# Attention of the first and last layer: values trail by three blocks; the ternary steps divided anew over the engines

## What is computed

```python
# layers 0 and 3, 16 heads of 16, 1024 tokens, per batch
scores = q @ k.T / 4
attn = softmax(where(causal, scores, -inf))
out = attn @ v            # layer 3 also multiplies by w_out and adds b_out

# layer 2, weights of the feed-forward branch, once for the whole run
def ternary_quant(w_fp32, g=64):
    w = w_fp32.astype(bfloat16)
    w_g = w.reshape(-1, g)
    scale = clip(mean(abs(w_g), axis=-1, keepdims=True), 1e-08, None)
    q = clip(round(w_g / scale), -1, 1)
    w_hat = (q * scale).reshape(w.shape)
    return w + stop_gradient(w_hat - w)
```

## Time and profile before

| what | value |
|---|---|
| runs, median (lowest to highest) | 4462.45 us (4454.85 to 4469.24), 3 runs |
| profiled execution, time | 4468.33 us |
| its span, first to last instruction | 4466.6 us |
| mean granted TensorE clock | 0.902 of full speed |
| PE busy | 3635.4 us, 81% |
| DVE busy | 2574.3 us, 58% |
| ACT busy | 1904.4 us, 43% |
| POOL busy | 850.4 us, 19% |

### The profile page before, as it was taken

One profiled execution on the slowest core, in us unless ns is written; L12 is line 12 of the kernel. 1 busy time (PEld: TensorE's weight loads), 2 busy tenths in 40 slices (PEclk: granted clock), 3 DMA queues, 4 the chain that ended last, 5 costly groups with the idle time before them and its releaser, 6 DMA issues. The chain is left out here.

```text
span 4466.6 us, 62749 instructions
## 1 busy us (share of the span) xinstructions
PE 3635.4 (81%) x23244; PEld 2181.8 (49%) x23244; DVE 2574.3 (58%) x5320; ACT 1904.4 (43%) x2923; POOL 850.4 (19%) x1022
## 2 busy tenths in 40 slices
PE   5776786768768888888893888987988888898897
PEld 3424333235166373554732666655653653663672
DVE  5756665647465454554546455455665665764764
ACT  2262461542656566464662434343126126216206
POOL 3012111120122030110302223232311220220220
PEclk8987897888889999898995989998999999999999
DMA  5411403214140000000002000002000000000000
GB/s 187 123 40 62 128 29 120 75 62 123 34 152 1 5 25 6 24 1 29 1 6 78 1 29 29 5 24 78 1 1 29 1 1 29 1 1 29 1 1 10
DMA packets 147087, 177.10 MB, mean 40 GB/s; under 512 B 16384, under 2 KB 123392, under 8 KB 146688
## 3 DMA queue, kind: packets, MB, share of 16 engines
q1 hardware_dynamic: 139008, 153.81, 10.9%
q0 software_dynamic: 6144, 16.79, 1.1%
q10 hardware_dynamic: 1632, 2.49, 0.2%
HBM read 126.40 MB, written 51.38 MB: 40 GB/s over the span
## 5 line engine op out<-in xcount | busy, mean ns | idle before, releaser
L708 DVE TENSOR_REDUCE arena<-ps 128x2 f32<-128x1024 f32 (+3 forms) x768 | 698.8, 953 | 170.6 <-PE ps L676 96.4
L906 ACT ACTIVATE arena<-ps 128x1024 f32<-128x1024 f32 (+3 forms) x768 | 576.6, 811 | 162.9 <-PE ps L813 111.8
L989 DVE TENSOR_TENSOR arena<-arena,tri 128x256 f32<-128x256 f32 x512 | 210.2, 423 | 354.5 <-ACT arena L906 325.2
L813 PE MATMUL ps<-arena 64*128 64x512 f16 (+3 forms) x1536 | 261.7, 355 | 163.3 <-ACT arena L906 99.0
L830 PE MATMUL ps<-arena 128*17 128x512 f32 (+3 forms) x3072 | 350.8, 531 | 6.4 <-DVE arena L989 4.1
L906 ACT ACTIVATE attention<-ps 128x1024 f32<-128x1024 f32 (+3 forms) x384 | 287.5, 810 | 142.7 <-PE ps L813 142.6
L2557 ACT ACTIVATE arena<-ps 128x256 f32<-128x256 f32 x192 | 63.6, 381 | 620.2 <-PE ps L2499 574.9
L813 PEld LDWEIGHTS ps<-arena 64*128 64x128 f16 x1536 | 71.1, 94 | 521.8 <-ACT arena L906 404.4
L830 PE MATMUL ps<-attention,live 128*33 128x512 f32 (+3 forms) x1536 | 290.8, 502 | 0.0
L676 PE MATMUL ps<-arena 64*128 64x512 f16 (+3 forms) x1536 | 238.2, 336 | 54.0 <-DVE arena L708 47.3
L1158 PE MATMUL ps<-gated_parts,weight_parts 128*128 128x256 f32 x1536 | 216.2, 298 | 30.4 <-DVE operands L1258 30.4
(11 more groups left out here) (324 smaller groups left out, 7094.6 us busy)
## 6 DMA issues: line engine op xcount, KB each, us to landing
arena<-w_experts SPq DMA_DIRECT2D x128, 256.0 KB
acc<-sums SPq DMA_DIRECT2D x16, 1024.0 KB, 5.9
x_next<-sums SPq DMA_DIRECT2D x16, 1024.0 KB, 8.5
arena<-slots_x SPq DMA_DIRECT2D x32, 512.0 KB, 4.6
slots_y<-arena SPq DMA_DIRECT2D x32, 512.0 KB, 4.3
sums<-acc SPq DMA_DIRECT2D x24, 512.0 KB, 2.9
making<-basis SPq DMA_DIRECT2D x16, 768.0 KB, 6.5
slots_x<-arena SPq DMA_DIRECT2D x1, 4096.0 KB, 29.5
```

The costliest lines, as they stand in the source:

```text
L708: dve.reduce_max(a.mp[:, 2 * j:2 * j + 2, qt, c], out[:, :, 0:w], AX.X).then_inc(self.pair_out, 1)
L813: last = pe.matmul(m.ps[:, 4 + 2 * (v % 2) + odd, q0:CH], a.k[half, pair, kt * P:(kt + 1) * P], a.q[half, pair, c * CH + q0:(c + 1) * CH], ...
L906: act.activation(a.p[:, v % ring, :, q0:CH], m.ps[:, b:b + 2, q0:CH], ACT.Exp, scale=HD ** -0.5).then_inc(exped, 1)
L989: dve.tensor_tensor(diag, diag, keep, ALU.min).then_inc(masked, 1)
```

## The change

In `attention` the lag becomes 3 where a group has two pairs (layers 0 and 3). The finishing pieces and `keep_sums` count from it and move one block later too.

In `ternary_weights` GpSimd's part goes, and VectorE does the last two steps for all three parts. ScalarE spreads the scale of a part over its 2048 columns into a new bf16 buffer, `f.spread`, and VectorE multiplies by that in place of the broadcast. There is one such buffer, so ScalarE waits for the part ahead (`ready`) before it fills it again.

```diff
@@ attention
-    lag = 2
+    lag = 3 if pairs == 2 else 2
@@ ternary_weights, VectorE
-                step(dve.tensor_scalar(f.sc[:, :], f.sc[:, :], 1e-8, None, ALU.max))
+                dve.tensor_scalar(f.sc[:, :], f.sc[:, :], 1e-8, None, ALU.max).then_inc(scale_made, 1)
+                dve.wait_ge(scale_made, i + 1)
...
-                dve.tensor_tensor(g3(q1), g3(q1), bc(f.sc[:, :]), ALU.mult).then_inc(scaled, 1)
-                dve.wait_ge(scaled, i + 1)
-                if i == last_part:
-                    dve.wait_ge(ready, last_part)
-                    step(dve.tensor_tensor(q1, q1, wb, ALU.subtract))
-                    dve.tensor_tensor(q1, q1, wb, ALU.add).then_inc(ready, 1)
-
-        @block.gpsimd
-        def _(pool):
-            for i in range(last_part):
-                wb, q1 = f.wb[:, i, :], f.q1[:, i, :]
-                pool.wait_ge(scaled, i + 1)
-                pool.tensor_tensor(q1, q1, wb, ALU.subtract).then_inc(lowered, 1)
-                pool.wait_ge(lowered, i + 1)
-                pool.tensor_tensor(q1, q1, wb, ALU.add).then_inc(ready, 1)
+                dve.wait_ge(scale_spread, i + 1)
+                step(dve.tensor_tensor(q1, q1, f.spread[:, :], ALU.mult))
+                step(dve.tensor_tensor(q1, q1, wb, ALU.subtract))
+                dve.tensor_tensor(q1, q1, wb, ALU.add).then_inc(ready, 1)
@@ ternary_weights, ScalarE
+            def spread(i):
+
+                act.wait_ge(scale_made, i + 1)
+                act.activation(f.spread[:, :].rearrange("p (g n) -> p g n", n=GROUP),
+                               f.sc[:, :].unsqueeze(2).broadcast_to([P, ng, GROUP]), ACT.Copy).then_inc(scale_spread, 1)
+
+            spread(0)
             for i in range(1, parts):
                 act.wait_ge(parts_in[i], parts_done)
                 act.activation(f.wb[:, i, :], f.raw[:, i, :], ACT.Copy).then_inc(cast, 1)
             for u in range(len(outs)):
+                if u == 0 or part_of[u] > part_of[u - 1]:
+                    if part_of[u] + 1 < parts:
+                        act.wait_ge(ready, part_of[u] + 1)
+                        spread(part_of[u] + 1)
```

More of the change, by code:

```diff
@@ L1776, in ternary_weights @@
     ng = f.raw.shape[2] // GROUP
-    with stage(nc, "steps", "cast", "scaled", "lowered", "ready", "turned", "stored", pool=True) as \
-            (block, steps, cast, scaled, lowered, ready, turned, stored):
-        last_part = parts - 1
+    with stage(nc, "steps", "cast", "scale_made", "scale_spread", "ready", "turned", "stored") as \
+            (block, steps, cast, scale_made, scale_spread, ready, turned, stored):
         @block.sync
@@ L2817, in program @@
                 f.raw = ar.take(3, part)
+                f.spread = ar.take(part, dtype=BF16)
                 f.wb = ar.take(3, part, dtype=BF16)
```

## The result

| what | before | after |
|---|---|---|
| median of 20 runs | 4461.98 us | 4473.43 us |
| lowest to highest | 4454.05 to 4476.48 us | 4464.66 to 4490.04 us |
| span of the profiled execution | 4466.6 us | 4474.9 us |
| mean granted TensorE clock | 0.902 | 0.902 |

The ratio is 1.0028, 95% interval 1.0017 to 1.0039: 11.5 us slower by the medians, where +2.2 was forecast. It lies inside the 0.3% that was called no change, and inside the range.

The account below looks back on a forecast made before the run. VectorE bounds `ternary_weights`; the slower of ScalarE and TensorE bounds each attention block. Second-chunk lag +9.1, first chunk +2 and ternary steps -8.9 us sum to +2.2: 4462.45 becomes 4464.6 us, range 4448 to 4478.

Parts of the forecast that it names:

- The ternary steps: In `ternary_weights`: 10.7 us of blocking and 3.2 of multiplication go, 5.0 of added steps come, 8.9 us less.
- Rival 4: In `ternary_weights`: the multiplication stays at 2.29 us despite the spread buffer, +3.2 us, 4468 us; chance 0.05.
- The plain group: Second chunk of attention, eight blocks without finishing pieces: the narrow 128 block holds wider values, +0.21 us.
- the groups with finishing: Layer 3, blocks 16 to 31, two groups of eight with finishing pieces moved one block later: +0.06 and +0.43 us.
- rival 1: Second chunk of attention: narrow blocks cost nothing, full blocks take the 0.2 us back, 4453 to 4458 us; chance 0.27.
- The tail: End of an attention stage: more values remain behind the last scores, which come 0.21 us later, +0.37 us.
- the low-clock stretches keep their length: Attention of layers 0 and 3: expected sign that TensorE's low-clock stretches get no longer; a longer one would disprove the forecast.
- rival 3: First chunk of each stage: the clock comes back later, 1.8 us a stage, 14 us in eight, 4479 us; chance 0.12.
- Layer 0's term: Layer 0, second chunk, blocks 16 to 23: the four turns move from blocks 19-22 to 20-23, +0.43 us.
- rival 2: First chunk of attention: it keeps its gain of 2.6 us a stage, up to 21 us in all eight; chance 0.12.
- the clock's rival: Another name for rival 3; the forecast range leaves out its far half.
- The likeliest case: Whole kernel: the forecast's own sum, +2.2 us to 4464.6 us, with its own range of 4459 to 4470; chance 0.44.

Follow-up runs that it names:

- the run with extra work: Changed kernel plus four unneeded TensorE products in each of blocks 41 and 42 of layer 3: 4355.68 against 4350.16 us, ratio 1.0014.
- the turns back: Changed kernel with the first chunk's finishing pieces left at their old blocks, from 19 on: 4366.12 us, one run.
- VectorE relieved: Changed kernel with layer 0's routed rows of tiles 4 to 7 in blocks 24 to 27 instead of 19 to 22: 4361.46 against 4350.16 us, ratio 1.0027.

## Why the prediction was right and wrong

**The ternary steps: right.** 8.9 us forecast, 9.1 measured, by the steps named: 0.18 us in all parts, 1.23 for the multiplication, 12.75 for a part where 12.9 was said, the spreading covered. Rival 4 fell.

**The second chunk's terms, layer 3: right in kind.** The plain group, forecast +0.21, has +0.29; the groups with finishing, forecast +0.06 and +0.43, have +0.12 and +0.30. Full blocks don't give back what a narrow block loses, so rival 1 fell. The tail, forecast +0.37 with the last group's own later scores: in the run with extra work, where the clock stays up, the last group has 12.99 against 12.67, +0.32, and from the last exponential to the copy it is 1.46 us in both kernels. So last group and tail together have +0.32 where the sum had +0.37. Without the low clock the four terms make 1.0 us a stage, where the sum had 1.1.

**The step that failed: "the low-clock stretches keep their length".** The sum took every product of the second chunk at full clock, since the rows of before had it. I looked at what each block costs, and not at how idle the change leaves TensorE in the blocks that cost nothing. With lag 3 TensorE has 2.08 us of work in 3.4 beside the narrow values, where it had 2.45. In layer 3's last group the clock falls behind it, and 1.2 us a stage follow, some four times the neighbouring terms. That it falls there and not at the equally idle places is not explained. Ahead of the root the low stretch grew from 3.4 to 6.8 us in three of the four stages of layer 3 and exponentials 20 to 32 take 12.8 us instead of 12.1. That is rival 3's mechanism, the clock coming back later, but with 0.7 us a stage instead of 1.8, and the larger part of it in a place that the rival didn't name. Behind the stages, where I had put nothing at all, another 7 us in four batches (17.4 - 10.4) went with further low stretches; that these are their cause is not shown. Together layer 3 has +17.4 us where the sum had 4.4.

**Layer 0's term was mis-sized**: +0.43 for blocks 16 to 23 became +1.54. The sum counted TensorE's pieces against ScalarE's blocks. It even noted that VectorE was 14.28 us busy of 15.73 and held a turn, and called that the same on both sides. It isn't: the turns' sums moved from block 19, which has no masks, to block 23, which has two, and there a block costs VectorE 2.80 us. The runs with the turns back (16.13) and with VectorE relieved (15.57) show it. Of the +2.6 us a stage that the lag alone costs in layer 0, 1.5 are this. The next group, forecast +0.21, has only +0.03 (13.30 to 13.33). The +0.5 that the sum gave the first chunk there is what it measured on the chips of the experiments, but by luck: it was put down to ScalarE's stalls, which these chips don't have, and came with the longer low stretch.

**The first chunk: rival 2 fell.** Exponential 20 starts 20.65 us behind the first scores in layer 3, 0.14 later than before in the second batch (20.51) and 0.26 earlier in the last (20.91 before): within the 0.3 that I gave it. What the masks' waits cost the values (4.1 us in 13 places) is gone from the waits, and nothing of it reached the end.

**The sum.** -9.1 for the ternary steps and, by the medians of the first chip, 11.5 + 9.1 = +20.6 for the lag, where 11 was forecast. The range held, because half of the clock's rival had been taken into it and what failed happened to be no larger; that is partly luck. The likeliest case, 4459 to 4470, didn't hold: the gain was right, and the lag cost nearly twice its forecast. What isn't settled is layer 0's share on that chip, whose stalls differ between the two profiles (12 and 8), and why each kernel's later low stretches fall where they do.

## What to carry to other kernels

When products are shifted against each other in a pipeline that another engine bounds, add up TensorE's busy time in each run of blocks after the shift, not only whether it is the bound in any of them: a stretch that becomes idler can lose the clock, and here one such stretch cost more (1.2 us a stage) than all the edges (1.0). Count a moved piece against every engine that takes part in it, in the block that it moves to. Two changes that go in together want a run each: here one gained 9 us, and the other cost at least twice that.

## What was unexpected

TensorE's clock fell to its lower level, 1.2 GHz, in the middle of a pipeline in which TensorE never stood for more than about 0.5 us at a time in the rows ahead. Products of no use, 8 in a stage, kept it at the upper one there, and the kernel with them took 4355.7 us where the changed one took 4366.5 on another chip, the kernel before being nearly equal on both (4350.2 and 4349.4).

Whether the clock falls depends on more than the work itself. With extra work only in blocks 7 to 9 the 84 us stretch vanished as well, with the same products around it. And in another execution of the changed kernel the last stage didn't have it, with the same 2.08 us of work at the place; its 3.4 us there, and its last group:

```profile
4338.90:4342.30 3.40, 2.08 (x24) 0.52 (x16) 0.69 (x1) 3.40 (x5) 0.00 (x0) 1.00 0.00 0
...
4337.28:4350.26 12.98, 11.20 (x98) 2.48 (x94) 3.87 (x9) 12.31 (x16) 0.00 (x0) 1.00 0.01 1
```

So the lag opened a place where the clock can fall. In layer 3's last group it did so in 3 or 4 of 4 stages, in the group ahead of it in none. What decides between the two stays open.

The same kernel took 4462 us on one chip and 4349.5 on three others, and the profile of the slower one books 46.6 us of ScalarE's waiting in layer 0 to a releaser that it calls remote. Its cause wasn't tried.
